# An iterated feed-forward block: eps is added to the sums of squares on GpSimd, and the variance operation on VectorE goes

## What is computed

```python
EPS = 1e-05
N_ITERS = 30
def _layernorm(x, w, bias):
    mu = jnp.mean(x, axis=-1, keepdims=True)
    var = jnp.mean(jnp.square(x - mu), axis=-1, keepdims=True)
    return (x - mu) * jax.lax.rsqrt(var + EPS) * w + bias
def step(h, _):
    h = h + 0.01 * jnp.tanh(h)
    h = h * jax.nn.sigmoid(h)
    h = _layernorm(h, ln_w, ln_b)
    h = jnp.einsum('bsc,dc->bsd', h, W) + b
    return (h, None)
```

## Time and profile before

| | us |
|---|---|
| median of 3 runs | 3121.51 (3121.39 to 3121.64) |
| the profiled execution | 3121.37 |
| its span in the trace | 3119.5 |
| busy: PE / PEld | 2528.0 / 2313.9 |
| busy: POOL | 2416.6 |
| busy: DVE | 2293.2 |
| busy: ACT | 1937.9 |

### The profile page before, as it was taken

The page is one execution under the profiler, slowest core; times in us unless marked ns, Lnnn a source line. Parts: engine busy times, 40 slices in busy tenths (PEclk is TensorE's granted clock), DMA queues, the critical chain, the costliest instruction groups (busy, mean ns, idle before and its releaser), DMA issues. The chain is left out here.

```text
span 3119.5 us, 56271 instructions
## 1 busy us (share of the span) xinstructions
PE 2528.0 (81%) x18717; PEld 2313.9 (74%) x18717; DVE 2293.2 (74%) x6189; ACT 1937.9 (62%) x2337; POOL 2416.6 (77%) x1775
## 2 busy tenths in 40 slices
PE   6799999999999449699999999998213977887782
PEld 6788888888888448588888888888202866676662
DVE  5799999999997445899999999997221444444441
ACT  4688888888884224788888888865101533333330
POOL 2499999999998638899999999986672666666666
PEclk9799999999999657799999999999556999999996
DMA  4000000000001311000000000001113655555551
GB/s 116 1 0 0 0 0 0 0 0 0 0 0 55 115 40 55 13 0 0 0 0 0 0 0 0 0 0 55 47 50 103 136 116 114 115 112 114 114 116 23
DMA packets 213939, 125.52 MB, mean 40 GB/s; under 512 B 30000, under 2 KB 200544, under 8 KB 213856
## 3 DMA queue, kind: packets, MB, share of 16 engines
q1 hardware_dynamic: 164192, 90.40, 10.4%
q0 software_dynamic: 49664, 34.15, 7.0%
HBM read 79.53 MB, written 47.03 MB: 41 GB/s over the span
## 5 line engine op out<-in xcount | busy, mean ns | idle before, releaser
L1112 PEld LDWEIGHTS ps<-w_ffn,turned 128*128 128x128 f32 x7680 | 1012.9, 192 | 36.6
L1112 PE MATMUL ps<-w_ffn,turned 128*128 128x128 f32 x7680 | 1015.9, 275 | 0.0
L469 POOL TENSOR_TENSOR it_rstd<-it_vars,minus_half 128x8 f32<-128x8 f32 x480 | 808.8, 1685 | 57.6 <-DVE it_vars L788 8.3
L475 POOL TENSOR_TENSOR scaled<-act_z,it_rstd 128x768 f32<-128x768 f32 x480 | 712.0, 1483 | 68.3
L641 DVE BATCH_NORM_STATS2 pair_stats<-act_z 128x6 f32<-128x256 f32 x1920 | 682.9, 415 | 0.0
L1101 PE MATMUL ps<-ident,scaled 128*128 128x128 f32 x4096 | 572.0, 284 | 111.6 <-DVE work L784 48.3
L983 ACT ACTIVATE act_z<-work 128x1024 f32<-128x1024 f32 x480 | 507.7, 1058 | 179.1 <-DVE work L784 179.0
L1101 PEld LDWEIGHTS ps<-ident,scaled 128*128 128x128 f32 x4096 | 453.7, 144 | 202.7 <-DVE work L784 152.8
L784 DVE SCALAR_TENSOR_TENSOR work<-work,ps 128x1024 f32<-128x1024 f32 x464 | 561.9, 1211 | 0.0
L565 POOL DMA_INDIRECT out_dram<-start_h,tokens_out x288 | 453.3, 1574 | 106.3 <-issue 106.3
L966 ACT COPY turned<-ps 128x1024 f32<-128x1024 f32 x480 | 486.4, 1013 | 58.1 <-PE ps L1101 35.1
(11 more groups left out here) (186 smaller groups left out, 2327.9 us busy)
## 6 DMA issues: line engine op xcount, KB each, us to landing
adjT<-in_L_ffn_W_dram SPq DMA_DIRECT2D x144, 256.0 KB
start_h<-sorted_rows SPq DMA_DIRECT2D x72, 264.0 KB
act_z<-in_adj_dram SPq DMA_DIRECT2D x16, 512.0 KB
resid<-in_x_dram SPq DMA_DIRECT2D x16, 512.0 KB, 5.2
out_dram<-resid SPq DMA_DIRECT2D x16, 512.0 KB, 3.8
scaled<-in_L_ffn_b_dram SPq DMA_DIRECT2D x72, 64.0 KB
out_dram<-start_h,tokens_out POOLq DMA_INDIRECT x288
sorted_rows<-start_h,slot POOLq DMA_INDIRECT x256
```

The costliest lines, as they stand in the source:

```text
L469: nc.gpsimd.tensor_tensor(it_rstd[:, c, :], it_vars[:, c, :], minus_half[:, 0:TILES], ALU.pow).then_inc(it_pow, 1)
L475: nc.gpsimd.tensor_tensor(scaled[c][:, 0:POOL_TILES, :], act_z[c][:, 0:POOL_TILES, :], wide(it_rstd[:, c, 0:POOL_TILES]), ALU.mult).then_i ...
L1112: last = nc.tensor.matmul(ps[c][:, t, :], stationary[:, t, :], moving(t), start=bias is None and m == 0, stop=m == len(terms) - 1, skip_gr ...
```

## The change

The variance operation on VectorE (L788) goes. `bn_stats` now signals `it_var` itself. GpSimd adds `EPS * 128` (a constant tile `eps_sum`) to the sums of squares, waits for that (`it_step`), and takes the power of the result. The factor 1/128 inside the root is made good by a factor sqrt(128) in `w_ffn`, once ahead of the loops.

```diff
+        eps_sum = sb("eps_sum", [P, TILES])
...
+            nc.gpsimd.memset(eps_sum[:, :], EPS * D)
...
                     pool.wait_ge(it_var, base + (k + 1))
+                    nc.gpsimd.tensor_tensor(
+                        it_vars[:, c, :].rearrange("p (i h) -> p i h", h=2),
+                        pair_stats[c][:, :, :].rearrange("p i (h e) -> p i h e", h=2)[:, :, :, 2],
+                        eps_sum[:, :].rearrange("p (i h) -> p i h", h=2), ALU.add).then_inc(it_step, 1)
+                    pool.wait_ge(it_step, base + (k + 1))
                     nc.gpsimd.tensor_tensor(it_rstd[:, c, :], it_vars[:, c, :], minus_half[:, 0:TILES],
                                             ALU.pow).then_inc(it_pow, 1)
...
-            nc.vector.tensor_copy(w_ffn[:, :], ps[0][:, 1, :])
+            nc.vector.tensor_scalar(w_ffn[:, :], ps[0][:, 1, :], float(D) ** 0.5, None, ALU.mult)
...
-                            pair_statistics(act_z[s % 4], s % 4).then_inc(it_step, 1)
+                            pair_statistics(act_z[s % 4], s % 4).then_inc(it_var, 1)
...
-                        if n is not None:
-                            dve.wait_ge(it_step, n + 1)
-                            nc.vector.tensor_scalar(
-                                it_vars[:, s % 4, :].rearrange("p (i h) -> p i h", h=2),
-                                pair_stats[s % 4][:, :, :].rearrange("p i (h e) -> p i h e", h=2)[:, :, :, 2],
-                                1.0 / D, EPS, ALU.mult, ALU.add).then_inc(it_var, 1)
```

## The result

| | before | after |
|---|---|---|
| median of 4 runs, us | 3121.57 (3121.39 to 3128.48) | 3162.84 (3160.18 to 3164.44) |
| the profiled execution / its span | 3121.37 / 3119.5 | 3163.20 / 3161.4 |
| busy POOL / DVE / ACT | 2416.6 / 2293.2 / 1937.9 | 2472.6 / 2329.8 / 1938.4 |

The changed kernel takes 1.0126 times as long as before, 95% interval 1.0108 to 1.0143: 41 us slower. The forecast was 3181 in 3155 to 3295.

What follows compares the result with a forecast made beforehand. GpSimd's sequence, with L788 in its one gap, was taken as the bound: 1.42 + 0.29 + 1.83 = 3.54 us against 3.407, +0.133 times 465 = +62 us, less 2 for small things, gave 3181 us, range 3155 to 3295.

Steps and rivals of the forecast that it cites:

- Who sets the period: Iteration loop: GpSimd's full queue, with L788 in its one gap, sets the 3.407 us period.
- The 3.12 us that TensorE "could do": TensorE in the loop: idling 0.29 us a step, it could run at a period of 3.12 us.
- The add and its wait, 0.29 us: New GpSimd add before the power: 0.29 us a step from add to power, priced from L545 to L546.
- the estimated 7: Surcharge for the add's 12-byte stride: an estimated 7 ns an operation, some 3 us in all, left out of the sum.
- Scaling to the next operation, 1.42: GpSimd's loop queue: start of scaling to start of the next operation falls from 1.58 to 1.42 us.
- Power to scaling, 1.83: GpSimd's loop queue: start of power to start of scaling stays 1.83 us, with 1.78 kept for the low end.
- The low-end sum of +39 us less 2: The loop's sum with power to scaling at 1.78: period 3.49, +0.083 us a step, +39 us; small things -2.
- the small things: Set-up memset, scaled copy of `w_ffn`, and the groups' first and last steps: -2 us for all.
- VectorE's free time: VectorE's free 0.68 us a step: its scaling pair gets held up by GpSimd's scaling, mean rising from 0.27 to about 0.6.
- Rival 1: GpSimd's add is locked out by VectorE's pair each step: +0.23 us a step, 3288 us; wholly or in part, chance 0.24.
- Rivals 2 and 3: GpSimd's add: 2, nearly free, 3098 us, chance 0.08; 3, no change, within 6 us of 3121, chance 0.05.
- the 0.16 us that "taking L788 away can give": GpSimd's wait for held-up L788 between scaling and power: 1.58 - 1.42 = 0.16 us a step, all its removal can give.

Runs made afterwards that it cites:

- e3: The changed kernel with VectorE also doing its old variance operation, into a tile nobody reads: +34.6 us against the kernel before (1.0109).
- e1: The changed kernel without the add and its wait, eps left out of the root: -101.6 us against the kernel before (0.9668).
- e6: The changed kernel with GpSimd's add done one stream early, between power and scaling: -99.5 us against the kernel before (0.9668).
- e8: The changed kernel with the add one stream early and GpSimd scaling 5 graphs instead of 6: -154.6 us against the kernel before (0.9489).
- e2: The kernel before, variance kept on VectorE, with an add of zero and a wait put ahead of GpSimd's power: +34.6 us against before (1.0112).
- e4: The kernel before with VectorE's variance operation moved ahead of its update, nothing added or removed: -101.8 us against before (0.9668).
- e5: The kernel before with an add of zero and its wait in each group's first 8 slots only, hardware loop unchanged: -92.8 us against before (0.9695).
- e7: The kernel before with the variance ahead of the update and GpSimd scaling 5 graphs instead of 6: -7.5 us against before (0.9968).

## Why the prediction held, and where it was off

**Who sets the period: right.** GpSimd's sequence does. Work put back on VectorE changed nothing (e3), work taken off GpSimd's path gave 0.28 us a step (e1, e6). The 3.12 us that TensorE "could do" was no floor, though: e8 ran at 3.09.

**The add and its wait, 0.29 us: right.** Measured 0.28 to 0.29, mean duration 0.204 us. The stride of 12 bytes, for which the Trainium skill (GPSIMD Engine Reference, Performance pitfalls for Q7 kernels) has a surcharge, can be seen as 203 ns against 199 for the contiguous add of e2, medians of 480 each: 4 ns, near the estimated 7. The two adds also differ in their operands, so no run isolates the stride.

**Scaling to the next operation, 1.42: right**, measured 1.43.

**Power to scaling, 1.83: this is the term that was mis-sized.** It is 1.78, the value kept for the low end: the power lasts 1.64 in the new order and not 1.69. That is 0.05 x 465 = 23 us, the distance from 3181 to the measured 3163 but for 5. The low-end sum of +39 us less 2 gives 3158. The rest is in the small things, put at -2 us: the first and last steps gave 4 us back, and some 6 us were added around the loops, which the prediction didn't have.

**VectorE's free time, right:** the hold-up moved to the pair, whose mean rose to 0.586 us (about 0.6 was forecast). The first of the two ends 0.08 us behind the scaling. Both together are held up by 2 x (0.586 - 0.273) = 0.63 us a step, which is all that VectorE has to spare at this period (3.49 - 2.86).

**Rival 1 (the add locked out each step) is refuted.** The add lasts 0.20 us in the median of its 480 instances and 0.224 at worst, though it starts at 604.43 with two VectorE scalings in flight until 604.75. The Trainium skill (SBUF — State Buffer, Who interferes with whom) has GpSimd and such VectorE operations block each other for whole instructions. The trace agrees for VectorE behind GpSimd. This add, with two such operations beside it, was not lengthened, and the first of them ended while the add ran.

**Rivals 2 and 3** fell with the 0.28 us.

**What was right in size but not in meaning** is the 0.16 us that "taking L788 away can give". It is 0.20 in e1 (3.41 to 3.21): 0.15 from scaling to power, and 0.05 from power to scaling, which the prediction left out there. And it is not L788's work that costs it. Moving L788 gives it (e4), and so does a nudge in the first slots (e5), and the add brings it along by itself (e2). The two halves of the change don't add up: -102 for the removal, +35 for the addition, +38 for both. The prediction's sum came out because in the new kernel the pair is the one held up, as it argued; its account of the kernel before as a fixed bound was incomplete. I had not seen that the same loop can also run at 3.21, or that GpSimd's queue of 3.20 us, found in pricing rival 2, was within reach of the kernel before.

## What to carry to other kernels

On the engine that sets the period, count the distance from start to start of every instruction, waits included. A 0.2 us operation with a wait behind it costs 0.28 us a step; the same operation put where the queue waits anyway costs nothing (e6). Where two engines hold each other up, ask which operation gets held up, and who needs its result next. If the next step needs it, put something between (move the operation, take its input a stream earlier), as the loop may otherwise settle into the slow order or the fast one by what happened in its first steps. Compare the period of like stretches of one trace, and compare it with the sum of the free spacings, before calling an engine the bound.

## What the runs showed of the hardware

**One loop, two periods.** The unchanged hardware loop of the kernel before ran at 3.41 or 3.21 us a step (before, e5), and one kernel ran at 3.13 in its first group and 3.67 in its second (e7). Each order kept itself up for over 200 steps.

**The power's length is not fixed.** The same 128x8 power lasts 1.64 us in most orders, 1.69 in the kernel before, and mostly 1.70 to 1.84 in runs with five graphs on GpSimd, where VectorE does three scalings a slot. In group 1 of e7, where no scaling of VectorE runs beside it, it is 1.64 again. But in e4 it is 1.64 with the end of such a pair beside it. Some collision lengthens it; which one stays open.

**A short GpSimd operation slips through, or doesn't.** The add at the end of GpSimd's own scaling lost nothing to the VectorE operations that were waiting for that end. The multiply of the earlier trace rows, with a long update of two SBUF inputs already running, lost 0.50 us. One add in the first slots of e8, beside the same kind of update, lost 0.41: it lasted 0.61 instead of 0.20 (L799 is the update).

```profile
137.56 1.23 DVE L799 SCALAR_TENSOR_TENSOR work<-work,start_h 128x1024 f32<-128x1024 f32 x1 [0.61 <-ACT work L985]
```
```profile
138.23 0.61 POOL L467 TENSOR_TENSOR it_vars<-pair_stats,eps_sum 128x8 f32<-128x8 f32 x1
```
